# Routed tiles of a mixture of experts: turned by the load's DMA instead of on TensorE

## The chip, the core and the metric

The kernel runs on one core of a Trainium2 chip. A core has TensorE (PE, the 128x128 matrix engine, which writes into PSUM), VectorE (DVE), ScalarE (ACT), GpSimd (POOL) and SyncE (SP, which here only issues transfers), and 16 DMA engines that they share. The engines run side by side and wait for one another through semaphores. The metric is the device time of one execution in microseconds; less is better.

## What is computed

A cross-attention block and then a transformer block with a mixture of experts, for 16 sequences of 128 tokens of width 256 (2,048 tokens). The change touches only the experts that a token is sent to. For each token the four largest of 16 routing weights are taken; each of the token's four experts computes a gated product, and the results are summed by weight:

```python
logits = x2 @ gate_w.T
probs = softmax(logits)
top_w, top_i = top_k(probs, 4); top_w = top_w / sum(top_w)
gu = einsum('th,eih->tei', x2, w1)          # 16 experts, 352 columns: gate | up
act = silu(gu[..., :176]) * gu[..., 176:]
down = einsum('tei,ehi->teh', act, w2)      # back to width 256
routed = einsum('te,teh->th', wfull, down)  # wfull: top_w at top_i, else 0
```

## The kernel before

Every float32 operand is split into a high and a low half of 16 bits, and a product is three products of halves (`three`, lines 666 to 670: high by high, high by low, low by high).

The kernel first does the attention of all sequences, group after group of four. While it does so, POOL scatters the rows of the tokens into a table `xg` in memory, sorted by expert (line 1536): a row holds the token's 256 high halves, its 256 low halves, and for the 16 experts the destination and the weight as 32 words, 1,152 bytes together. A short stage for the shared experts' products follows, and then the stage that the change touches.

That stage takes the sorted rows in 80 slots of 128 rows (tiles), 79 of them in use, each of one expert; two tiles are a pair, and 40 pairs (`PAIRS`) are worked through. For pair u:

- SP loads the pair's tiles from `xg` into one of four buffers `xin` (`load`, line 637; the issue is line 644). It may do so when TensorE has turned the pair four before (`tx_free`) and DVE has written that pair's destinations (`idx`).
- TensorE turns them (`turn_tile`, line 1067): the products need the 256 columns on the partitions, so four 128x128 blocks a tile are transposed into one PSUM bank (line 1076), and DVE copies them to `xt`, of which there are two (`take`, line 2118, the copy is line 2123).
- DVE picks the destination and the weight of the pair's expert out of the 32 words (`select`, lines 2130 and 2135) and later writes them where the scatter and the store read them (`index`, lines 2144 and 2145), when POOL has seen the scatter of the pair four before land (`y_free`).
- TensorE makes gate and up (`gate_up`, line 1086, 12 products a pair through lines 668 to 670).
- ACT takes tanh of the gate (line 1408), DVE multiplies twice (`expert`, lines 2150 and 2152), ACT cuts the product to its high half (line 1414), DVE makes the low half (`lo_tile`, lines 2157 and 2158).
- TensorE turns the product (`turn_m`, line 1107), ACT copies it (line 1420), TensorE makes the down products (`down_tile`, lines 668 to 670, 1119 and 1120), ACT stores them times the weight (line 1428), and POOL scatters the rows to their destinations in `y4` (`send`, line 1594).

Each engine has its own fixed order, written out by hand. TensorE for pair u: gate and up of u, turn of u+2, down of u-2, turn of the product of u-1. ACT: tanh of u, cut of u, copy of u-1, store of u-2. DVE: the two multiplications of u, index of u, copy of u+2 (`take`), selection for u+2, low part of u. After the last pair SP loads `y4` back, and DVE adds the four results of each token and the rest.

Of the kernel before, what the change touches and what calls it, by code (L numbers as in the profile page):

```python
# [9 lines left out]
F32, F16, BF16 = mybir.dt.float32, mybir.dt.float16, mybir.dt.bfloat16  # L10
U32, I32 = mybir.dt.uint32, mybir.dt.int32

P = 128
NB, S, D = 16, 128, 256
KC = D // P
# [7 lines left out]
NE, EI, TOPK = 16, 176, 4  # L23
# [6 lines left out]
GU = 2 * EI  # L30
# [19 lines left out]
PAIRS = NT // 2  # L50
# [5 lines left out]
RW = 2 * D + 4 * NE  # L56
# [8 lines left out]
CH = SHL * NC  # L65
TC = 17
HID = 2048
ATT = HID + 1024
# [61 lines left out]
def build(nc, x, yT, wa, wall, cst, ident, maskb, pad, xg, y4, zb, x1d, x2t, out):  # L130
    assert (WRES - NH * HW) % SMALL == 0 and sum(CUTS) == NH
    with ExitStack() as ctx:
# [5 lines left out]
        def sem(name):  # L138
            if name not in sems:
                sems[name] = ctx.enter_context(nc.semaphore(name))  # L140
            return sems[name]
# [9 lines left out]
        def apart(eng):  # L151


            eng.sem_inc(sem("apart"), 1)
# [36 lines left out]
        idn, tri, ones = (idn2[:, n * P:(n + 1) * P] for n in range(3))  # L191

        def words(a, n):
            return ar[:, a:a + n]

        def halves(a, n):
            return ar[:, a:a + n].bitcast(F16)

        def bank16(b, n=1):
            return ps[:, b:b + n, :].rearrange("p b w -> p (b w)").bitcast(F16)  # L200

        def bank(b, n=1):
            return ps[:, b:b + n, :].rearrange("p b w -> p (b w)")
# [136 lines left out]
        def wcol(w, off, n=P):  # L340
            return w[:, bass.ds(off, n)]
# [20 lines left out]
        nt_i = tab[:, 4 * NT + 3 * NE:4 * NT + 4 * NE].bitcast(I32)  # L362
        grid = words(ATT, NT * NE).rearrange("p (t e) -> p t e", e=NE)
        up16 = words(ATT + NT * NE, NE * NE).rearrange("p (f e) -> p f e", e=NE)
        xin = [halves(ATT + RW * b, RW).rearrange("p (i c) -> p i c", i=2) for b in range(4)]
        xinw = [words(ATT + RW * b, RW).rearrange("p (i c) -> p i c", i=2) for b in range(4)]
        xt = [halves(ATT + 4 * RW + 512 * b, 512).rearrange("p (l k t) -> p l k t", l=2, k=KC) for b in range(2)]
        m_t = [words(ATT + 3328 + 448 * b, 2 * EI).rearrange("p (i n) -> p i n", i=2) for b in range(2)]
        m_p = [words(512 * b, 2 * EI).rearrange("p (i n) -> p i n", i=2) for b in range(2)]
        m_s = [halves(RT + 384 * b, 384).rearrange("p (i n) -> p i n", i=2) for b in range(2)]  # L370
# [3 lines left out]
        selw = [words(ATT + 4224 + 72 * b, 72) for b in range(2)]  # L374
        yb = [(whi, wlo)[m // 4][:, LATE0 + 4096 * (m % 4):LATE0 + 4096 * (m % 4 + 1)].bitcast(F32) for m in range(NB // 2)]
        ob = [words(ATT + 512 * m, 512) for m in range(NB // 2)]
        GUB, TXB, MB, DB = (0, 2), 4, 5, (6, 7)
        gate_ps = [ps[:, GUB[b]:GUB[b] + 2, 0:EI] for b in range(2)]
        up_ps = [ps[:, GUB[b]:GUB[b] + 2, EI:GU] for b in range(2)]

# [65 lines left out]
        def unit_at(slot):  # L446

            return slot - slot // 3 if slot % 3 != 2 and slot < SMALL * 3 // 2 else None
# [24 lines left out]
        def tiles(u):  # L473

            return min(2, LIVE - 2 * u)
# [12 lines left out]
        def _(sp):  # L488
# [82 lines left out]
            for p in range(LAST):  # L571
# [20 lines left out]
                if p >= FIRST:  # L592
                    g, t = divmod(p - FIRST, GB)
                    if t == 2:
                        load_x1(g)
                    for n in range(GB):
                        u = unit_at((p - FIRST) * GB + n)
# [38 lines left out]
            def load(u, v, again=True):  # L636

                if again:
                    sp.wait_ge(sem("tx_free"), u + 1)
                    sp.wait_ge(sem("idx"), u - 3)  # L640
                both = sp.value_load(rowtab[0:1, u:u + 1], min_val=0, max_val=512 * 512 - 1)
                for i, r in enumerate((both & 511, both >> 9)[:tiles(u)]):
                    r = (r * P).with_bounds(min_val=0, max_val=SLOTS - P)
                    sp.dma_start(xinw[v][:, i, :], xg[bass.ds(r, P), :]).then_inc(sem(f"xin{v}"), 16)

            for u in range(PAIRS):
                load(u, u % 4, u >= 4)
# [14 lines left out]
        def _(pe):  # L662
# [3 lines left out]
            def three(o, l_hi, l_lo, r_hi, r_lo, start, stop):  # L666

                mm(o, l_hi, r_hi, start=start, stop=False, skip_group_check=True)  # L668
                mm(o, l_hi, r_lo, start=False, stop=False, skip_group_check=True)  # L669
                return mm(o, l_lo, r_hi, start=False, stop=stop, skip_group_check=True)  # L670
# [389 lines left out]
            s_down(2, 2)  # L1060

            pe.wait_ge(sem("fin"), SHL)
            pe.sem_inc(sem("tx_free"), 4)
            pe.sem_inc(sem("u_ps"), 2)
            pe.sem_inc(sem("d_ps"), 2)

            def turn_tile(u, v, n):

                pe.wait_ge(sem(f"xin{v}"), n)
                pe.wait_ge(sem("tx_bank"), u + 1)  # L1070
                t = bank16(TXB).rearrange("p (l k t) -> p l k t", l=2, k=KC)
                for i in range(tiles(u)):
                    for l in range(2):
                        for k in range(KC):
                            o = (l * KC + k) * P
                            last = nc.tensor.transpose(t[:, l, k, i * P:(i + 1) * P], xin[v][:, i, o:o + P], idn)  # L1076
                last.then_inc(sem("tx_free"), 1)

            word = {}

            def fetch(n):

                if n < NT // 4:
                    word[n] = pe.value_load(exptab[0:1, n:n + 1], min_val=0, max_val=16 ** 4 - 1)

            def gate_up(u, b):

                off = [((word[u // 2] >> 4 * (2 * (u % 2) + i)) & 15) * ES + LATE0 for i in range(2)]
                pe.wait_ge(sem("tx_bank"), u + 2)
                pe.wait_ge(sem("me_v"), u + (CH + 2))  # L1090
                for i in range(tiles(u)):
                    tt = slice(i * P, (i + 1) * P)
                    for k in range(KC):
                        last = three(bank(GUB[b] + i)[:, 0:GU], xt[b][:, 0, k, tt], xt[b][:, 1, k, tt],
                                     wcol(whi, off[i] + k * GU, GU), wcol(wlo, off[i] + k * GU, GU),
                                     k == 0, k == KC - 1)
                last.then_inc(sem("u_ps"), 1)
                return off

            def turn_m(u, b):  # L1100

                pe.wait_ge(sem("me_lo"), u + (CH + 3))
                pe.wait_ge(sem("mT_cut"), u)
                o = bank16(MB)[:, 0:6 * P].rearrange("p (c i t) -> p c i t", c=3, i=2)
                for i in range(tiles(u)):
                    for n in range(3):
                        last = nc.tensor.transpose(o[:, n, i, :], m_s[b][:, i, n * P:(n + 1) * P], idn)  # L1107
                last.then_inc(sem("mt_ps"), 1)
# [14 lines left out]
            pe.wait_ge(sem("stage_cut"), NH + SMALL + 1 + LATE)  # L1123
            pe.wait_ge(sem("table"), 3)
            fetch(0)
            for u in range(2):
                turn_tile(u, u, 32)
            off = {}
            for u in range(PAIRS + 2):
                if u < PAIRS:  # L1130
                    off[u] = gate_up(u, u % 2)
                if u + 2 < PAIRS:
                    turn_tile(u + 2, (u + 2) % 4, 32 * ((u + 2) // 4) + 16 * tiles(u + 2))
                if u % 2:
                    fetch(u // 2 + 1)
                if u >= 2:
                    down_tile(u - 2, u % 2, off[u - 2])
                if 1 <= u <= PAIRS:
                    turn_m(u - 1, (u - 1) % 2)
# [477 lines left out]
        def _(dve):  # L1617
            prime(dve, "dve")
            V = nc.vector
# [491 lines left out]
            s_add(2)  # L2111
            r_z(g)

            dve.sem_inc(sem("tx_bank"), 1)
            dve.sem_inc(sem("me_lo"), 1)
            dve.sem_inc(sem("me_v"), 2)

            def take(u, b):

                dve.wait_ge(sem("tx_free"), u + 5)  # L2120
                dve.wait_ge(sem("u_ps"), u + (CH + 1))
                apart(dve)
                V.tensor_copy(xt[b].rearrange("p l k t -> p (l k t)"), bank16(TXB)).then_inc(sem("tx_bank"), 1)

            def select(u, v, n):

                b = v % 2
                dve.wait_ge(sem(f"xin{v}"), n)
                for i in range(2):
                    last = STT(selw[b][:, 32 * i:32 * i + 32].rearrange("p (w e) -> p w e", w=2),  # L2130
                               cs[:, C_IOTA:C_IOTA + NE].unsqueeze(1).broadcast_to([P, 2, NE]), etab[:, 2 * u + i:2 * u + i + 1],
                               xinw[v][:, i, D:D + 2 * NE].rearrange("p (w e) -> p w e", w=2), ALU.is_equal, ALU.mult)
                last.then_inc(sem("dve_step"), 1)
                dve.wait_ge(sem("dve_step"), 2 * u + (NG * RC + TC + 1))
                V.tensor_reduce(selw[b][:, 64:68], selw[b][:, 0:64].rearrange("p (i e) -> p i e", i=4),
                                AX.X, ALU.add).then_inc(sem("dve_step"), 1)
# [24 lines left out]
            for b in range(2):  # L2161
                V.memset(m_s[b][:, :, EI:2 * P], 0.0)
            for u in range(2):
                take(u, u)
                select(u, u, 32)
            for u in range(PAIRS):
                expert(u, u % 2)
                index(u, u % 4)
                if u + 2 < PAIRS:
                    take(u + 2, u % 2)  # L2170
                    select(u + 2, (u + 2) % 4, 32 * ((u + 2) // 4) + 16 * tiles(u + 2))
                lo_tile(u, u % 2)

# [125 lines left out]
```

## Time and the profile before

| | |
|---|---|
| time before, median of three runs | 987.31 us (984.85 to 988.54) |
| span of the profiled execution | 989.1 us |
| time of the profiled execution outside its span | not given |
| mean granted TensorE clock | 0.910 |
| instructions | 24,025 |
| DMA | 83.81 MB, 85 GB/s on average |

The span is the time from the first to the last instruction. The clock is given as a share of full speed, 2.4 GHz. In the rows of the profile, L1076 is line 1076 of the kernel; PE is a product on TensorE, PEld its load of weights; SPq is SP's queue. `ar`, `ps`, `whi` and `wlo` are the names of buffers: `ar` holds nearly all that is worked on, `ps` is PSUM, `whi` and `wlo` the weights' halves. A bracket such as [0.77 <-ACT ar L1408] says how long the engine stood idle ahead of the instruction and what ended the wait. Matmuls are pipelined, so their lengths overlap; the distance from one start to the next is the rate.

### The profile page before, as it was taken

How to read it: one execution, taken by the hardware profiler on the slowest of the kernel's cores; microseconds unless marked ns; L12 is line 12 of the kernel's file. 1: busy time of each engine (PE TensorE's matmuls, PEld its weight loads, DVE VectorE, ACT ScalarE, POOL GpSimd, SP SyncE). 2: the span in 40 equal slices, each digit the busy share in tenths (PEclk: the TensorE clock that was granted, in tenths of full speed). 3: DMA queues.
4: the chain of work that ended last, by engine and by line, in shares of the span. 5: the costliest groups of instructions: out<-in, count | busy, mean ns of one | idle time of the engine just before them, and what ended most of it. 6: DMA issues, size and time to landing. Idle time of an engine off the chain costs nothing. (4 is left out here: it accounts for less than half of the span.)

```text
span 989.1 us, 24025 instructions
## 1 busy us (share of the span) xinstructions
PE 861.2 (87%) x8118; PEld 611.6 (62%) x8118; DVE 794.5 (80%) x2309; ACT 664.4 (67%) x1611; POOL 516.8 (52%) x607
## 2 busy tenths in 40 slices
PE   3476689999999898999999899998998579999971
PEld 1243346777767676676767677676765357787740
DVE  4688878888888988989998877778867767777738
ACT  3677878888888877788788676666753136666640
POOL 5778883466466463777745264211453715554540
PEclk8555559999999999999999999999999779999986
DMA  5222320101001010122000223114231534444448
GB/s 183 93 77 75 102 104 23 31 19 43 15 25 30 23 52 1 59 87 71 26 15 9 65 91 119 39 34 134 80 103 46 189 108 150 153 155 148 137 161 316
DMA packets 47493, 83.81 MB, mean 85 GB/s; under 512 B 6144, under 2 KB 36224, under 8 KB 47328
## 3 DMA queue, kind: packets, MB, share of 16 engines
q1 hardware_dynamic: 39504, 61.45, 19.7%
q0 software_dynamic: 6864, 19.80, 5.7%
q8 instruction: 69, 1.13, 0.5%
q10 hardware_dynamic: 1008, 1.03, 0.3%
q14 instruction: 48, 0.39, 0.1%
HBM read 52.77 MB, written 31.85 MB: 86 GB/s over the span
## 5 line engine op out<-in xcount | busy, mean ns | idle before, releaser
L668 PE MATMUL ps<-whi,ar 128*128 128x256 f16 (+1 forms) x797 | 225.9, 283 | 19.0 <-DVE ar L1764 9.4
L670 PE MATMUL ps<-whi,ar 128*128 128x256 f16 (+1 forms) x797 | 225.6, 283 | 0.0
L669 PE MATMUL ps<-wlo,ar 128*128 128x256 f16 (+1 forms) x797 | 225.6, 283 | 0.0
L1543 POOL TENSOR_TENSOR ar<-ar,sm 128x512 f32<-128x512 f32 x64 | 69.8, 1090 | 149.2 <-DVE sm L1833 149.1
L668 PE MATMUL ps<-ar 128*128 128x128 f16 (+1 forms) x768 | 117.4, 207 | 13.0 <-issue 5.3
L1458 POOL TENSOR_TENSOR sm<-sm,mhalf 128x1 f32<-128x1 f32 (+2 forms) x72 | 125.4, 1741 | 6.0
L1594 POOL DMA_INDIRECT y<-ar,idx x79 | 76.0, 962 | 88.3 <-ACT ar L1428 74.4
L669 PE MATMUL ps<-ar 128*128 128x128 f16 (+1 forms) x768 | 117.0, 206 | 0.0
L670 PE MATMUL ps<-ar 128*128 128x128 f16 (+1 forms) x768 | 117.0, 206 | 0.0
L668 PE MATMUL ps<-ar,whi 128*128 128x512 f16 x292 | 114.3, 392 | 0.2
L669 PE MATMUL ps<-ar,whi 128*128 128x512 f16 x292 | 114.2, 391 | 0.0
L670 PE MATMUL ps<-ar,wlo 128*128 128x512 f16 x292 | 113.9, 390 | 0.0
L668 PEld LDWEIGHTS ps<-whi,ar 128*128 128x128 f16 x797 | 78.6, 99 | 43.3 <-DVE ar L1764 10.2
L1507 POOL TENSOR_TENSOR ar<-ar 128x512 f16<-128x512 f32 x64 | 78.6, 1230 | 49.9 <-ACT ar L1212 49.8
L1268 ACT ACTIVATE ar<-ps 128x512 f16<-128x512 f32 x128 | 76.8, 601 | 34.7 <-PE ps L670 33.4
L1799 DVE SCALAR_TENSOR_TENSOR ar<-ps,ar 128x512 f16<-128x512 f32 x128 | 86.3, 678 | 15.8 <-ACT ar L1268 14.6
L1292 ACT ACTIVATE ar<-ps,sm 128x128 f32<-128x128 f32 x256 | 90.7, 377 | 0.8
L668 PEld LDWEIGHTS ps<-ar 128*128 128x128 f16 x768 | 72.1, 98 | 28.4 <-issue 19.6
L670 PEld LDWEIGHTS ps<-whi,ar 128*128 128x128 f16 x797 | 78.6, 99 | 15.8
L669 PEld LDWEIGHTS ps<-wlo,ar 128*128 128x128 f16 x797 | 78.5, 99 | 15.5
L1536 POOL DMA_INDIRECT xg<-xrow,rn x64 | 67.7, 1057 | 16.8 <-issue 15.6
L1826 DVE CUSTOM_DVE_ANT_0 ps<-ps,msk 128x128 f32<-128x128 f32 x256 | 66.3, 320 | 12.3 <-PE ps L670 11.2
(234 smaller groups left out, 2308.0 us busy)
## 6 DMA issues: line engine op xcount, KB each, us to landing
ar<-xg SPq DMA_DIRECT2D x79, 144.0 KB
ar<-in_wall SPq DMA_DIRECT2D x16, 512.0 KB, 3.6
stg<-in_wall SPq DMA_DIRECT2D x32, 188.0 KB, 2.5
ar<-in_wall SPq DMA_DIRECT2D x8, 608.0 KB, 4.3
whi<-y SPq DMA_DIRECT2D x4, 1024.0 KB, 8.1
wlo<-y SPq DMA_DIRECT2D x4, 1024.0 KB, 16.0
xg<-in_pad SPq DMA_DIRECT2D x1, 2304.0 KB
xg<-x1d SPq DMA_DIRECT2D x4, 512.0 KB, 4.7
```

Of the source, the lines that this page charges most:

```text
L668: mm(o, l_hi, r_hi, start=start, stop=False, skip_group_check=True)
L669: mm(o, l_hi, r_lo, start=False, stop=False, skip_group_check=True)
L670: return mm(o, l_lo, r_hi, start=False, stop=stop, skip_group_check=True)
L1268: A(qkT[:, w, 0, :], bank(QKV[b]), ACT.Copy, scale=(-QK_SCALE, QK_SCALE)[w]).then_inc(sem(("q_hi", "k_hi")[w]), 1)
L1292: last = A(pr[:, j, :], bank(SB_)[:, j * S:(j + 1) * S], ACT.Exp, bias=nm4[:, j:j + 1], scale=-1.0, accum_out=es4[:, j:j + 1])
L1458: TT(out, tmp, mhalf[:, 0:w], ALU.pow).then_inc(sem(name + "_rs"), 1)
L1507: TT(to[:, 1].rearrange("p h q -> p (h q)"), of, to[:, 0].rearrange("p h q -> p (h q)"), ALU.subtract).then_inc(sem("xa_pl"), 1)
L1536: nc.gpsimd.indirect_dma_start(out=xg, out_offset=bass.IndirectOffsetOnAxis(ap=pos[:, n:n + 1], axis=0), in_=xrow[:, (n // TOPK) * (RW // ...
L1543: TT(pr, pr, er4.unsqueeze(2).broadcast_to([P, GB, S]), ALU.mult).then_inc(sem("p_n"), 1)
L1594: nc.gpsimd.indirect_dma_start(out=y4, out_offset=bass.IndirectOffsetOnAxis(ap=idx[:, 2 * v + i:2 * v + i + 1], axis=0), in_=ybuf[v][:, i, ...
L1799: STT(qkT[:, w, 1, :], bank(QKV[b]), (-QK_SCALE, QK_SCALE)[w], qkT[:, w, 0, :], ALU.mult, ALU.subtract).then_inc(sem(("q_lo", "k_lo")[w]), 1)
L1826: last = V.tensor_tensor_reduce(bank(SB_)[:, c], bank(SB_)[:, c], msk[:, :], 1.0, -MASKED, ALU.add, ALU.min, nm4[:, j:j + 1])
```

## The change

SP's load of a tile becomes two DMAs. The first, a transposing one, reads the 512 halves of each of the tile's 128 rows and writes them with columns on partitions, straight into `xt`, of which there are now four. The second reads the 32 words of destinations and weights of each row into `xmeta`. TensorE's `turn_tile` and DVE's `take` go; `gate_up` waits for the load itself, and a buffer is free for the next load when `gate_up` of the pair four before is done.

```diff
-        xin = [halves(ATT + RW * b, RW)... for b in range(4)]
-        xinw = [words(ATT + RW * b, RW)... for b in range(4)]
-        xt = [halves(ATT + 4 * RW + 512 * b, 512)... for b in range(2)]
+        xmeta = [words(ATT + 4 * NE * b, 4 * NE).rearrange("p (i c) -> p i c", i=2) for b in range(4)]
+        xt = [halves(ATT + 16 * NE + 512 * b, 512).rearrange("p (l k t) -> p l k t", l=2, k=KC) for b in range(4)]
+        xt_c = [halves(ATT + 16 * NE + 512 * b, 512).rearrange("p (c t) -> p c t", c=2 * KC) for b in range(4)]
+        xg16 = xg.bitcast(F16)
...
             def load(u, v, again=True):
                 if again:
-                    sp.wait_ge(sem("tx_free"), u + 1)
+                    sp.wait_ge(sem("u_ps"), u + (CH - 1))
                     sp.wait_ge(sem("idx"), u - 3)
...
-                    sp.dma_start(xinw[v][:, i, :], xg[bass.ds(r, P), :]).then_inc(sem(f"xin{v}"), 16)
+                    sp.dma_start_transpose(xt_c[v][:, :, i * P:(i + 1) * P], xg16[bass.ds(r, P), 0:2 * D]).then_inc(
+                        sem(f"xin{v}"), 16)
+                    sp.dma_start(xmeta[v][:, i, :], xg[bass.ds(r, P), D:D + 2 * NE]).then_inc(sem(f"xin{v}"), 16)
...
-            def turn_tile(u, v, n):
-                pe.wait_ge(sem(f"xin{v}"), n)
-                pe.wait_ge(sem("tx_bank"), u + 1)
-                t = bank16(TXB).rearrange("p (l k t) -> p l k t", l=2, k=KC)
-                for i in range(tiles(u)):
-                    for l in range(2):
-                        for k in range(KC):
-                            o = (l * KC + k) * P
-                            last = nc.tensor.transpose(t[:, l, k, i * P:(i + 1) * P], xin[v][:, i, o:o + P], idn)
-                last.then_inc(sem("tx_free"), 1)
...
-            def gate_up(u, b):
+            def gate_up(u, b, v, n):
-                pe.wait_ge(sem("tx_bank"), u + 2)
+                pe.wait_ge(sem(f"xin{v}"), 2 * n)
                 pe.wait_ge(sem("me_v"), u + (CH + 2))
-                        last = three(bank(GUB[b] + i)[:, 0:GU], xt[b][:, 0, k, tt], xt[b][:, 1, k, tt],
+                        last = three(bank(GUB[b] + i)[:, 0:GU], xt[v][:, 0, k, tt], xt[v][:, 1, k, tt],
...
-                if u + 2 < PAIRS:
-                    turn_tile(u + 2, (u + 2) % 4, 32 * ((u + 2) // 4) + 16 * tiles(u + 2))
...
-            def take(u, b):
-                dve.wait_ge(sem("tx_free"), u + 5)
-                dve.wait_ge(sem("u_ps"), u + (CH + 1))
-                V.tensor_copy(xt[b].rearrange("p l k t -> p (l k t)"), bank16(TXB)).then_inc(sem("tx_bank"), 1)
             def select(u, v, n):
-                dve.wait_ge(sem(f"xin{v}"), n)
+                dve.wait_ge(sem(f"xin{v}"), 2 * n)
...
-                               xinw[v][:, i, D:D + 2 * NE].rearrange("p (w e) -> p w e", w=2), ALU.is_equal, ALU.mult)
+                               xmeta[v][:, i, :].rearrange("p (w e) -> p w e", w=2), ALU.is_equal, ALU.mult)
...
-                    take(u + 2, u % 2)
```

## Rows read from the trace of the kernel before

**Rows 1.** The page's busy times, share of the span and instructions of each engine.
```profile
PE 861.2 (87%) x8118; PEld 611.6 (62%) x8118; DVE 794.5 (80%) x2309; ACT 664.4 (67%) x1611; POOL 516.8 (52%) x607
```
**Rows 2.** Groups by line from 740 us on: busy us, mean ns | idle before.
```profile
L2123 DVE COPY ar<-ps 128x1024 f16<-128x1024 f16 x40 | 27.4, 684 | 5.1 <-PE ps L1076 5.0 <-issue 0.2
L1076 PE MATMUL ps<-idn,ar 128*128 128x128 f16 x316 | 25.0, 224 | 7.2 <-DMA ar<-xg 5.8 <-DVE ar L2123 1.3
```
**Rows 3.** Stretches of the stage: length, busy time by engine, clock, DMA share, GB/s.
```profile
858.43:936.57 78.14, 77.72 (x760) 61.47 (x758) 59.80 (x210) 50.54 (x106) 40.29 (x42) 1.00 0.49 150
936.57:943.43 6.86, 6.20 (x59) 4.74 (x57) 4.79 (x16) 4.58 (x11) 3.84 (x4) 1.00 0.19 68
```
**Rows 4.** Timeline of TensorE in one pair: start, length, what.
```profile
817.78 0.31 PE L670 MATMUL ps<-whi,ar 128*128 x1
817.93 0.61 PE L1076 MATMUL ps<-idn,ar 128*128 128x128 f16 x8
818.38 0.27 PE L668 MATMUL ps<-whi,ar 128*128 x1
...
819.81 0.31 PE L668 MATMUL ps<-whi,ar 128*128 x1
```
**Rows 5.** Timeline of ACT in the same pair.
```profile
814.47 0.46 ACT L1408 ACTIVATE ar<-ps 128x352 f32<-128x352 f32 x1
816.08 0.50 ACT L1414 ACTIVATE ar<-ar 128x352 f16<-128x352 f32 x1 [1.14 <-DVE ar L2152]
...
817.17 0.84 ACT L1428 ACTIVATE ar<-ps,wt 128x256 f32<-128x256 f32 x2
818.13 0.46 ACT L1408 ACTIVATE ar<-ps 128x352 f32<-128x352 f32 x1
```
**Rows 6.** Timeline of DVE in the same pair.
```profile
818.63 0.52 DVE L2150 SCALAR_TENSOR_TENSOR ar<-ar,ps 128x352 f32<-128x352 f32 x1 [0.77 <-ACT ar L1408]
...
819.76 0.68 DVE L2123 COPY ar<-ps 128x1024 f16<-128x1024 f16 x1
...
822.29 0.52 DVE L2150 SCALAR_TENSOR_TENSOR ar<-ar,ps 128x352 f32<-128x352 f32 x1 [0.77 <-ACT ar L1408]
```
**Rows 7.** Timeline of ACT in the last pairs.
```profile
936.57 0.46 ACT L1408 ACTIVATE ar<-ps 128x352 f32<-128x352 f32 x1
...
940.01 0.47 ACT L1408 ACTIVATE ar<-ps 128x352 f32<-128x352 f32 x1
...
942.71 0.83 ACT L1428 ACTIVATE ar<-ps,wt 128x256 f32<-128x256 f32 x2
943.43 0.47 ACT L1408 ACTIVATE ar<-ps 128x352 f32<-128x352 f32 x1
```
**Rows 8.** Timeline of TensorE in the last pairs.
```profile
942.95 0.28 PE L668 MATMUL ps<-whi,ar 128*128 x1 [0.66 <-ACT ar L1420]
```
**Rows 9.** DMA queues, 810 to 930 us: packets, MB, share of 16 engines.
```profile
q1 hardware_dynamic: 9327, 9.56, 27.5%
q0 software_dynamic: 3069, 8.39, 20.6%
```
**Rows 10.** The same around a load of 128 rows of 512 bytes, 109.05 to 109.60 us.
```profile
q1 hardware_dynamic: 144, 0.07, 41.6%
```
**Rows 11.** Line 644's instructions on SP: duration ns, smallest, median, largest.
```profile
L644 SPq DMA_DIRECT2D ar<-xg x79: 332/333/1344, 791.9 to 932.3; - x79
```
**Rows 12.** Timeline of all engines where the stage starts.
```profile
791.90 6.16 SPq L644 DMA_DIRECT2D ar<-xg  x8
...
794.75 1.04 PE L1076 MATMUL ps<-idn,ar 128*128 128x128 f16 x8 [5.83 <-DMA ar<-xg]
...
797.61 0.50 PE L668 MATMUL ps<-whi,ar 128*128 x1
```
**Rows 13.** Waits from 780 to 950 us: us in total, times, longest.
```profile
DVE wt L2144 <- POOLq L1601: 1.9, 4, 1.1
```
**Rows 14.** Timeline of POOL in one pair.
```profile
820.08 0.96 POOL L1594 DMA_INDIRECT y<-ar,idx  x1 [0.30 <-issue]
```

More of the change, by code:

```diff
@@ L364, in build @@
         up16 = words(ATT + NT * NE, NE * NE).rearrange("p (f e) -> p f e", e=NE)
-        xin = [halves(ATT + RW * b, RW).rearrange("p (i c) -> p i c", i=2) for b in range(4)]
-        xinw = [words(ATT + RW * b, RW).rearrange("p (i c) -> p i c", i=2) for b in range(4)]
-        xt = [halves(ATT + 4 * RW + 512 * b, 512).rearrange("p (l k t) -> p l k t", l=2, k=KC) for b in range(2)]
+        xmeta = [words(ATT + 4 * NE * b, 4 * NE).rearrange("p (i c) -> p i c", i=2) for b in range(4)]
+        xt = [halves(ATT + 16 * NE + 512 * b, 512).rearrange("p (l k t) -> p l k t", l=2, k=KC) for b in range(4)]
+        xt_c = [halves(ATT + 16 * NE + 512 * b, 512).rearrange("p (c t) -> p c t", c=2 * KC) for b in range(4)]
+        xg16 = xg.bitcast(F16)
         m_t = [words(ATT + 3328 + 448 * b, 2 * EI).rearrange("p (i n) -> p i n", i=2) for b in range(2)]
@@ L376, in build @@
         ob = [words(ATT + 512 * m, 512) for m in range(NB // 2)]
-        GUB, TXB, MB, DB = (0, 2), 4, 5, (6, 7)
+        GUB, MB, DB = (0, 2), 5, (6, 7)
         gate_ps = [ps[:, GUB[b]:GUB[b] + 2, 0:EI] for b in range(2)]
@@ L1062, in _ @@
             pe.wait_ge(sem("fin"), SHL)
-            pe.sem_inc(sem("tx_free"), 4)
             pe.sem_inc(sem("u_ps"), 2)
             pe.sem_inc(sem("d_ps"), 2)
-            def turn_tile(u, v, n):
-                pe.wait_ge(sem(f"xin{v}"), n)
-                pe.wait_ge(sem("tx_bank"), u + 1)
-                t = bank16(TXB).rearrange("p (l k t) -> p l k t", l=2, k=KC)
-                for i in range(tiles(u)):
-                    for l in range(2):
-                        for k in range(KC):
-                            o = (l * KC + k) * P
-                            last = nc.tensor.transpose(t[:, l, k, i * P:(i + 1) * P], xin[v][:, i, o:o + P], idn)
-                last.then_inc(sem("tx_free"), 1)
             word = {}
@@ L1125, in _ @@
             fetch(0)
-            for u in range(2):
-                turn_tile(u, u, 32)
             off = {}
@@ L1130, in _ @@
                 if u < PAIRS:
-                    off[u] = gate_up(u, u % 2)
-                if u + 2 < PAIRS:
-                    turn_tile(u + 2, (u + 2) % 4, 32 * ((u + 2) // 4) + 16 * tiles(u + 2))
+                    off[u] = gate_up(u, u % 2, u % 4, 32 * (u // 4) + 16 * tiles(u))
                 if u % 2:
@@ L2112, in _ @@
             r_z(g)
-            dve.sem_inc(sem("tx_bank"), 1)
             dve.sem_inc(sem("me_lo"), 1)
             dve.sem_inc(sem("me_v"), 2)
-            def take(u, b):
-                dve.wait_ge(sem("tx_free"), u + 5)
-                dve.wait_ge(sem("u_ps"), u + (CH + 1))
-                apart(dve)
-                V.tensor_copy(xt[b].rearrange("p l k t -> p (l k t)"), bank16(TXB)).then_inc(sem("tx_bank"), 1)
             def select(u, v, n):
                 b = v % 2
-                dve.wait_ge(sem(f"xin{v}"), n)
+                dve.wait_ge(sem(f"xin{v}"), 2 * n)
                 for i in range(2):
@@ L2163, in _ @@
             for u in range(2):
-                take(u, u)
                 select(u, u, 32)
```

## The prediction

> **What bounds the kernel now.** I read the page first. TensorE is busy in 87% of the span, far above the other engines [rows 1], but that is an average over stages. The change touches only the stage of the routed tiles, 40 pairs from about 791 to 949 us, so I took the table of stretches next. In its middle TensorE is busy for 77.72 of 78.14 us, at full clock (1.00, the 2.4 GHz level), while DVE has 59.80 and ACT 50.54 [rows 3]. TensorE has no idle time there, so taking work from it should help. How much depends on who is next.
>
> For that I read the timeline of one pair, engine by engine. TensorE: the last product of gate and up starts at 817.78, the eight turns of the pair after next at 817.93, the down products at 818.38, the next gate and up at 819.81 [rows 4]. The turns take 818.38 - 817.93 = 0.45 us. ACT: tanh of one pair starts at 814.47, of the next at 818.13; the period is 3.66 us [rows 5]. In between it does the cut, the copy of the turned products and the store, and before the cut it stands 1.14 us waiting for DVE's two multiplications, every time. The store ends at 817.17 + 0.84 = 818.01, the next tanh starts at 818.13, and the last gate product that it needs ends at 817.78 + 0.31 = 818.09. So ACT, at 60% busy, waits for TensorE by only about 0.1 us. The reader should see this: ACT does its four steps strictly in order, with DVE's 1.14 us inside, and this loop is nearly as long as TensorE's.
>
> How long it is without TensorE the trace shows itself. The last pairs have nothing left to turn. There tanh starts at 936.57, 940.01 and 943.43 [rows 7], 3.44 and 3.42 us apart, and now TensorE waits for ACT, 0.66 us before a down product [rows 8]. The last of them starts 0.11 us before the store's end (942.71 + 0.83 = 943.54): ACT is full. So the pace without turns is 3.43 us: TensorE alone would allow 3.66 - 0.45 = 3.21.
>
> **The change part by part.**
>
> *Turns removed.* 316 transposes [rows 2], 0.45 us a pair of TensorE's time. Worth on the path: 3.66 - 3.43 = 0.23 us a pair, because ACT's loop ends later than TensorE's shortened one. The first two pairs and the last two differ, so I count 35 periods: 35 x 0.23 = 8.0 us. From 814.47 to 936.57 there are 33 periods in 122.10 us, 3.70 on average [rows 5, 7]; the 0.04 above 3.66 comes from a few disturbed pairs, and I leave it in place. Bounds: 0 (ACT doesn't give more) to 35 x 0.45 = 15.8 (ACT follows TensorE fully), and the two measured intervals of 3.43 lie between. TensorE will then idle some 0.2 us a pair; in the stretch of those last pairs it is busy for 6.20 of 6.86 us and the clock is 1.00 [rows 3], so I price the clock at nothing.
>
> *DVE's copy removed.* 40 copies of 0.68 us [rows 2]. DVE isn't on the path: it stands 0.77 us in each pair waiting for tanh [rows 6]. Price nothing; but the cover for anything late on DVE grows from 0.77 to 1.45 us.
>
> *Loads become transposing DMAs.* The trace has none, so this is the unknown. What a plain load costs: in 810 to 930 us the SP queue took 27.5% of the 16 engines' 120 us for 9,327 packets [rows 9]; at 144 packets a load (128 rows and 16 that end it, as in [rows 10]) these are 64.8 loads, 0.51 us of all engines each, 57 ns a packet of 1,152 bytes. The scatter of the results takes 20.6%, two for each pair: 0.206 x 120 / 32 = 0.77 us a pair. Now each of a row's four pieces of 128 halves goes to 128 partitions, so I reckon with pieces of 256 bytes: 512 a tile, 32 for each engine. Below: as dear by the byte as the plain load, 128/144 x 0.51 = 0.45 us a tile. Above: each piece as dear as one packet of 1,152 bytes, 32 x 57 ns = 1.82 us. Nearest row: packets of 512 bytes, 0.55 us x 41.6% over 9 packets for each engine = 25.4 ns [rows 10], so 32 x 25.4 = 0.81 us. I take that, because small packets are the likeness that counts.
>
> The plain row, 0.51 us a load, speaks for cheap tiles [rows 9]; it says nothing of crossing partitions. One rule of the Trainium skill speaks against the change: "VectorE: DVE Perf Modes", section The three transpose paths, gives 1,309 ns for one 128x128 block of 2-byte elements by DMA. An estimate from that page: eight blocks a pair, one behind another, would take 10.5 us, and the sum would end some 260 us above today's time. No trace here shows it; the same mechanism, priced from rows, stands among the rivals.
>
> *The small DMAs.* Two more for each pair, 128 pieces of 128 bytes: below, by the byte, next to nothing; at 25.4 ns a packet 9 x 25.4 = 0.23 us each; above, at 57 ns, 0.51.
>
> *All four on the DMA engines.* 2 x (0.81 + 0.23) + 0.77 = 2.85 us a pair, under 3.43; now it is 2 x 0.51 + 0.77 = 1.79. Lowest 2 x 0.45 + 0.77 = 1.67, highest 2 x (1.82 + 0.51) + 0.77 = 5.43.
>
> *SP's issue.* It issues in order, 0.333 us a DMA [rows 11], some 0.45 with the register work. Four instead of two: 1.8 us a pair, beside 3.43; were each transposing issue as long as the longest plain one (1.344), 3.6, about today's period. SP's wait for the index of the pair four before stands as it was, and its other wait is for gate and up in place of the turns. Nothing else is queued behind these on SP until the stage ends.
>
> *When it is needed.* A load goes out when the index of the fourth pair before is done, and DVE's selection for it comes two periods later, 6.9 us. Two plain tiles landed 794.75 - 791.90 = 2.85 us after the first issue [rows 12]; with two more issues and 2 x 0.3 us more on the engines it is about 4.4. So 2.5 us are in hand, and DVE's 1.45 us behind them: selection stands ahead of the low parts on DVE, and TensorE's turning of the products waits for these.
>
> *The start.* The first gate product started at 797.61, 5.71 us after the first issue [rows 12], behind two turns of about 1 us and two copies. With four issues and a landing it may start 4.4 us after; if the tiles cost their upper bound, about 6.5. I take -0.5, with ends of -1.5 and +1.
>
> **Sum.** -8.0 - 0.5 = -8.5 us. The profiled execution's span is 989.1 us, 1.8 above the median of the runs, 987.31; no other time of that execution is given. I put the difference on the median: 987.3 - 8.5 = 979 us, 0.9% faster.
>
> **Rivals.**
>
> *The DMAs can't keep the pace (slower).* The place is SP's queue: gate and up waits for the tile, all else behind it. It decides where a pair's transfers pass today's 3.66 us: (3.66 - 0.77)/2 - 0.23 = 1.2 us a tile, 2.4 times the plain load. For it: 512 pieces instead of 128, crossing partitions, and a queue in which each small DMA stands behind a tile. Against it: the engines are idle half the time now (0.49) [rows 3], and the 512-byte packets were cheap. At 4.9 us a pair (1.82 a tile) it is 38 x 1.24 = 47 us more, 1,034; at the upper bound 5.43, 38 x 1.77 = 67, 1,054. A form of it: a tile's four blocks pass one behind another, each as dear as a whole plain load, 4 x 0.51 = 2.04 a tile, 2 x (2.04 + 0.23) + 0.77 = 5.31 a pair and 1,050. I give that form 0.10 of this rival's 0.30. It is the one that the page named above would bear out, with a far higher price.
>
> *The scatters land later and take the gain.* DVE's index waits until the scatter of the fourth pair before has landed; already it waited in four pairs, 1.9 us in total [rows 13]. The scatter's second issue ends at 820.08 + 0.96 = 821.04 [rows 14], and the landing comes just in time. Tiles of many small pieces on the same 16 engines could delay it. DVE's 1.45 us hide that much; a landing 1.7 us later costs 0.25 a pair and leaves 987, and 2.5 later gives 1.05 a pair against 3.43: 4.48, or 987 + 38 x 0.82 = 1,018. Against it: a scatter is few and large packets, 0.39 us of engine time each.
>
> *ACT's loop gives nothing.* Then TensorE's 0.45 us turn into waits for ACT and the time is 987. The two intervals of 3.43 speak against it, but they are only two.
>
> **How the numbers follow.** About 0.5% (5 us) is what a measurement of this kernel can tell from no change. Forecast: 0.60, of which 0.50 is faster by over 0.5% and 0.10 is a gain that stays under it. DMAs too slow: 0.30, of which 0.28 slower and 0.02 just hidden. Scatters late or ACT's loop holding: 0.10, of which 0.06 same and 0.04 slower. So faster 0.50, same 0.18, slower 0.32. The forecast's own range is 975 to 984 (start and pace at their ends). The whole range must reach into the slow case: 975 to 1,045 leaves out 0.03 below and about 0.12 above.
>
> **What would show it.** Right: no turns on TensorE in the stage, tanh 3.4 us apart, ACT without a gap between store and tanh, TensorE idle some 0.2 us a pair and waiting for ACT's copy, the stage about 8 us shorter, and everything after it unchanged. Wrong: gate and up waiting for a DMA in every pair, tanh at even distances over 3.66 us, SP's queue full. If instead DVE's index waits for POOL's queue in each pair, the second rival holds; if tanh stays 3.66 us apart with ACT full, the third.

## The result and the profile after

The change makes the kernel slower: 1,034.95 us, median of four runs (1,032.12 to 1,041.13), against 986.08 us (984.52 to 988.54) for the kernel before on the same chip. The ratio is 1.0489, 95% interval 1.0455 to 1.0523. I had forecast 979 us, faster; the time lies in the range of 975 to 1,045, where the first rival put it, though not for that rival's reason.

The profiled execution, the slowest of the four (1,041.13 us), spans 1,039.3 us. Busy times on its page, to be held against [rows 1]:

```profile
span 1039.3 us, 23429 instructions
PE 867.8 (84%) x7802; PEld 596.4 (57%) x7802; DVE 773.8 (74%) x2269; ACT 661.6 (64%) x1611; POOL 513.9 (49%) x607
```

TensorE has 316 instructions fewer, which are the turns, and DVE 40 fewer, the copies. TensorE's busy time still rose by 6.6 us, and the last section comes back to that.

**Where the time went.** tanh (L1394 now) starts 40 times, first at 799.34 and last at 993.60 us, (993.60 - 799.34) / 39 = 4.981 us apart on average. Before it was 801.36 to 943.43, or 3.643. So 39 x 1.338 = 52.2 us were lost in the pairs' pace, 2.0 us won at the start, and 50.2 us is the whole difference of the spans, 1,039.3 - 989.1. Behind the last tanh both traces have the same 45.7 us.

The stretch in the middle of the stage (length, busy time of PE, PEld, DVE, ACT, POOL, clock, DMA share, GB/s), to be held against the first row of [rows 3], and a second, short one inside it:

```profile
830.00:950.00 120.00, 93.68 (x689) 62.68 (x687) 56.13 (x220) 56.34 (x123) 46.28 (x48) 0.93 0.50 113
855.00:862.00 7.00, 5.06 (x31) 3.46 (x32) 3.98 (x16) 2.39 (x5) 2.82 (x4) 0.76 0.41 99
```

No engine is full any more: TensorE 78%, DVE 47%, ACT 47%. Nor are the DMA engines, at 0.50, about the share they had before (0.49). When nothing that computes or moves is full, the next thing to look at is who waits for whom. The waits from 780 to 1,000 us (total, times, longest):

```profile
DVE ar L2108 <- DMA ar<-xg: 103.4, 40, 4.0
ACT ar L1400 <- DVE ar L2130: 94.4, 38, 4.0
...
PE ps L1097 <- DVE ar L2136: 43.6, 26, 3.2
...
PE ps L671 <- DMA ar<-xg: 7.0, 2, 5.9
```

The DMA is waited for in every pair, and by DVE's selection (L2108), not by gate and up (L671, only twice). One such wait on DVE, TensorE and ACT:

```profile
865.54 0.41 DVE L2108 SCALAR_TENSOR_TENSOR ar<-cs,tab,ar 128x32 f32<-128x32 f32 x2 [3.06 <-DMA ar<-xg]
...
866.13 0.42 DVE L2135 TENSOR_TENSOR ar<-ar 128x256 f16<-128x256 f32 x1
866.46 0.25 DVE L2136 TENSOR_TENSOR ar<-ar 128x96 f16<-128x96 f32 x1
866.63 0.52 DVE L2128 SCALAR_TENSOR_TENSOR ar<-ar,ps 128x352 f32<-128x352 f32 x1
```

```profile
866.77 0.51 PE L1097 MATMUL ps<-idn,ar 128*128 128x128 f16 x6 [1.55 <-DVE ar L2136]
```

```profile
867.74 0.50 ACT L1400 ACTIVATE ar<-ar 128x352 f16<-128x352 f32 x1 [3.08 <-DVE ar L2130]
```

DVE stands 3.06 us at the selection for a pair that nobody computes on yet. Behind it in DVE's order are the low part of the current pair (L2135, L2136), for which TensorE's turn of the product waits, and the two multiplications of the next (L2128, L2130), for which ACT's cut waits. One late tile stops three engines.

Why is it late? SP's timeline over one pair, its lines over the stage (smallest, median, longest ns), and what SP itself waited for from 795 to 930 us:

```profile
839.55 1.21 SPq L645 DMA_TRANSPOSE ar<-xg  x1
840.96 0.42 SPq L647 DMA_DIRECT2D ar<-xg  x1
841.56 1.20 SPq L645 DMA_TRANSPOSE ar<-xg  x1
842.95 0.43 SPq L647 DMA_DIRECT2D ar<-xg  x1
844.27 1.21 SPq L645 DMA_TRANSPOSE ar<-xg  x1
```

```profile
L645 SPq DMA_TRANSPOSE ar<-xg x79: 1188/1211/2421, 790.1 to 984.6; - x79
...
L647 SPq DMA_DIRECT2D ar<-xg x79: 389/427/1824, 791.6 to 986.0; - x79
...
L642 SPq TENSOR_LOAD <-tab x40: 268/276/528, 789.3 to 983.8; - x40
```

```profile
SPq L642 <- PE ps L673: 0.8, 2, 0.5
```

SP waits for 0.8 us in these 135 and is never done. Issuing one transposing DMA occupies it for 1.21 us, against 0.333 for the plain load of before [rows 11]. A pair takes 844.27 - 839.55 = 4.72 us on SP alone: 2 x 1.21 + 2 x 0.43 = 3.28 in the four issues and 1.44 in the steps between them (the pair's word, L642, and the addresses). Pairs in which an issue or a word load is stretched bring the average to 4.98. The chain that ended last says the same, by line:

```profile
SPq L645 9%; SPq L647 4%; SPq L642 2%; POOL xg L1522 2%; DMA ar<-xg 1%; PE ps L671 1%; PE ps L672 1%; PE ps L673 1%; DVE ar L2156 1%; DVE ar L2163 1%; DVE whi L2154 0%; DVE wlo L2154 0%; PE ps L1097 0%; DMA xg<-xrow,rn 0%; DVE ar L2108 0%
```

Could the 1.21 us be SP held up by full DMA engines? The queues from 830 to 950 us, to be held against [rows 9], and the first issues of the stage:

```profile
q1 hardware_dynamic: 33066, 7.09, 31.3%
q0 software_dynamic: 2304, 6.29, 17.9%
```

```profile
790.07 1.32 SPq L645 DMA_TRANSPOSE ar<-xg  x1
...
791.59 0.41 SPq L647 DMA_DIRECT2D ar<-xg  x1
792.20 1.20 SPq L645 DMA_TRANSPOSE ar<-xg  x1
```

The first issue of the stage, with no tile in flight ahead of it, is no shorter than the others (1.32).

### The profile page after: what moved, and what is told of

It is laid out like the page before. It is cut to its first block and busy times, and to the rows that moved or that the text cites. A ratio compares the mean times of both kernels' runs of the same rounds, so it can differ in the third digit from the quotient of the medians.

```text
span 1039.3 us, 23429 instructions
## 1 busy us (share of the span) xinstructions
PE 867.8 (84%) x7802; PEld 596.4 (57%) x7802; DVE 773.8 (74%) x2269; ACT 661.6 (64%) x1611; POOL 513.9 (49%) x607
## 5 line engine op out<-in xcount | busy, mean ns | idle before, releaser
L671 PE MATMUL ps<-whi,ar 128*128 128x256 f16 (+1 forms) x797 | 232.7, 292 | 25.9 <-DVE ar L1750 9.6
L672 PE MATMUL ps<-wlo,ar 128*128 128x256 f16 (+1 forms) x797 | 232.1, 291 | 0.0
L673 PE MATMUL ps<-whi,ar 128*128 128x256 f16 (+1 forms) x797 | 231.7, 291 | 0.0
L671 PE MATMUL ps<-ar 128*128 128x128 f16 (+1 forms) x768 | 117.3, 207 | 13.6 <-issue 5.3
L671 PEld LDWEIGHTS ps<-whi,ar 128*128 128x128 f16 x797 | 80.3, 101 | 63.6 <-issue 22.4
L671 PE MATMUL ps<-ar,whi 128*128 128x512 f16 x292 | 114.5, 392 | 0.2
L2108 DVE SCALAR_TENSOR_TENSOR ar<-cs,tab,ar 128x32 f32<-128x32 f32 x80 | 16.7, 250 | 103.4 <-DMA ar<-xg 103.4
L673 PEld LDWEIGHTS ps<-whi,ar 128*128 128x128 f16 x797 | 80.6, 101 | 17.3
L671 PEld LDWEIGHTS ps<-ar 128*128 128x128 f16 x768 | 72.1, 98 | 28.8 <-issue 20.0
L1400 ACT ACTIVATE ar<-ar 128x352 f16<-128x352 f32 x40 | 19.9, 497 | 97.3 <-DVE ar L2130 94.4
```

## The experiments

Two theories. A: SP's queue is full, because the issue of a transposing DMA holds it for 1.2 us. B: the transfer itself is slow, small pieces that cross partitions on the DMA engines, as my first rival had it. All kernels start from the changed one. Times are medians, ratios are to the kernel before on the same chip.

**Same pieces, plain DMA.**

```diff
-                    sp.dma_start_transpose(xt_c[v][:, :, i * P:(i + 1) * P], xg16[bass.ds(r, P), 0:2 * D]).then_inc(
+                    sp.dma_start(xt_c[v][:, :, i * P:(i + 1) * P],
+                                 xg16[bass.ds(r, P), 0:2 * D].rearrange("p (c t) -> p c t", t=P)).then_inc(
```

> The transposing DMA is replaced by a plain one of the same rows in the same pieces (256 bytes on both sides), so the tile arrives unturned and the products are made from the wrong layout: only the time is read. Theory A (SP's queue is full, because the issue of one transposing DMA holds SP for 1.2 us): four plain issues of 0.43 us, some 0.2 around each and 0.5 for the table word make about 3.0 us a pair on SP, under ACT's loop of 3.43, so the time is what the prediction said for the removed turns alone, 979 us (975 to 984), with tanh 3.43 us apart. Theory B (the 512 pieces a tile on the 16 DMA engines set the pace, and SP's records are long because the engines push back): the pieces are the same, so at least 1,020 us.

Measured: 975.59 us (973.06 to 976.61), ratio 0.9861 (0.9833 to 0.9889). tanh from 797.21 to 932.10 us, 3.459 apart on average, median 3.42. The issues, and the middle of the stage:

```profile
L645 SPq DMA_DIRECT2D ar<-xg x79: 383/383/1437, 789.5 to 921.4; - x79
```

```profile
800.00:930.00 130.00, 126.75 (x1045) 90.36 (x1046) 86.76 (x340) 83.92 (x184) 67.53 (x71) 1.00 0.61 155
```

The kernel leaves the turning out, so only its time is read. The same number of DMAs, bytes and 256-byte pieces, with another issue: the loss is gone. What is left is the pace that I had forecast, 3.42 for 3.43, with TensorE at full clock. It leaves room for crossing partitions as the price, since these pieces don't cross; the next two kernels settle that.

**Small DMAs issued by ACT.** SP keeps the transposing DMAs and nothing else; ACT issues the small ones behind tanh, three pairs ahead, on semaphores of their own.

```diff
-                    sp.dma_start(xmeta[v][:, i, :], xg[bass.ds(r, P), D:D + 2 * NE]).then_inc(sem(f"xin{v}"), 16)
...
+            def meta(u, v):
+                if u >= 4:
+                    act.wait_ge(sem("idx"), u - 3)
+                both = act.value_load(rowtab[0:1, u:u + 1], min_val=0, max_val=512 * 512 - 1)
+                for i, r in enumerate((both & 511, both >> 9)[:tiles(u)]):
+                    r = (r * P).with_bounds(min_val=0, max_val=SLOTS - P)
+                    act.dma_start(xmeta[v][:, i, :], xg[bass.ds(r, P), D:D + 2 * NE]).then_inc(sem(XM[v]), 16)
```

> The small DMAs are issued from ACT, three pairs ahead, in the 1.1 us that ACT waits for DVE in each pair; the transposing ones stay on SP. Theory A: SP has two issues of 1.2 us, 0.2 around each and about 0.85 for word, waits and registers, 3.65 us a pair instead of 4.7 to 4.9, so 990 to 998 us. Theory B: the same transfers cross the same engines, so it stays near 1,035 (over 1,025). If ACT's queue can't hide the issues, its loop grows to about 4.3 us, 1,010 to 1,020, with ACT and not SP without a gap.

Measured: 983.23 us (981.76 to 985.01), ratio 0.9951 (0.9929 to 0.9972). tanh 3.637 apart on average, median 3.42, from 795.12 to 936.98. The issues, and the queues from 810 to 930 us (q10 is ACT's):

```profile
L646 SPq DMA_TRANSPOSE ar<-xg x79: 1188/1191/2607, 786.7 to 929.1; - x79
```

```profile
q1 hardware_dynamic: 35362, 8.53, 40.8%
q0 software_dynamic: 3105, 8.52, 24.1%
q10 hardware_dynamic: 9310, 1.06, 12.1%
```

The transfers are those of the changed kernel; only the engine that issues the small ones is another, and with it their queue. 51.7 us came back, and the ratio fell from 1.0489 to 0.9951. The 79 issues, 786.7 to 929.1 us, are 142.4 / 78 = 1.83 us apart, 3.65 a pair, which is what theory A gave for SP, and tanh keeps that average. The engines were busier than in the changed kernel, 0.77 (the sum of the three rows) against 0.50, at a much better pace: they had not been the limit. The time itself is a miss: it lies under A's 990 to 998 us, although A's pace held. The range did not follow from that pace, since 39 x (4.98 - 3.65) = 51.9 us off 1,034.95 is 983. The stage also began earlier here (first issue at 786.7, not 790.1), for a reason that I don't know.

**Each transposing DMA cut in two**, of 64 rows each.

```diff
-                    sp.dma_start_transpose(xt_c[v][:, :, i * P:(i + 1) * P], xg16[bass.ds(r, P), 0:2 * D]).then_inc(
-                        sem(f"xin{v}"), 16)
+                    for h in range(2):
+                        sp.dma_start_transpose(xt_c[v][:, :, i * P + HALF * h:i * P + HALF * h + HALF],
+                                               xg16[bass.ds(r + HALF * h, HALF), 0:2 * D]).then_inc(sem(f"xin{v}"), 16)
```

> Each transposing DMA is split into two of 64 rows; pieces and bytes stay the same. Theory A: the issue on SP decides. If its 1.2 us is a fixed price, four of them with 0.2 each, two small ones and the word make 7.7 us a pair, about 1,145 us; if it goes by the blocks moved, 0.6 each, about 5.2 us a pair and 1,050 to 1,060; so in either case slower than the change, by how much tells the fixed part. Theory B: the same pieces, the same time, 1,035 (1,028 to 1,042).

Measured: 1,139.78 us (1,138.48 to 1,141.40), ratio 1.1528 (1.1496 to 1.1560), tanh 7.505 apart on average. The issues, and the queues from 830 to 1,070 us:

```profile
L646 SPq DMA_TRANSPOSE ar<-xg x158: 1169/1176/2292, 791.7 to 1088.6; - x158
```

```profile
q1 hardware_dynamic: 45648, 9.38, 20.0%
q0 software_dynamic: 3001, 8.17, 10.1%
```

Half the rows cost SP 1.18 us instead of 1.21: the price goes by the DMA, not by its bytes. It decides between the theories, for the bytes are unchanged, the engines are no busier, and the time is 105 us longer.

**One tile of each pair turned by DMA, the other on TensorE.** Tile 0 keeps the transposing and the small DMA, tile 1 comes by the plain load of before, with four turns and half a copy, so that SP has one dear issue a pair. All three DMAs of a pair count on one semaphore.

```diff
+                if tiles(u) == 2:
+                    sp.dma_start(xinw[v], xg[bass.ds(rows[1], P), :]).then_inc(sem(f"xin{v}"), 16)
+                for i, r in enumerate(rows[:1]):
...
+                for l in range(2):
+                    for k in range(KC):
+                        o = (l * KC + k) * P
+                        last = nc.tensor.transpose(t[:, l, k, :], xin[v][:, o:o + P], idn)
```

> Of each pair one tile comes by the transposing DMA with its small DMA, the other by the plain load of before and four turns on TensorE with half the copy on DVE. Theory A: SP needs 0.43 + 1.4 + 0.6 + 0.85 = 3.3 us a pair, TensorE 3.66 - 0.22 = 3.44, ACT 3.43, so about 981 us (977 to 988), faster than both kernels. Theory B: transport of 0.5 + 2.4 us or so a pair would also fit in 3.44, so it says the same here; a time over 1,000 would speak against A.

Measured: 997.65 us (993.77 to 1,003.78), ratio 1.0097 (1.0066 to 1.0129), a miss. About half of the pairs go at 3.44 (the median is 3.53), but the average is 3.964: some take 4.3 to 7.55. The waits of the turn from 795 us on, and one of them on TensorE with ACT's copy behind it:

```profile
PEld ps L1082 <- DMA ar<-xg: 15.6, 17, 2.1
...
PE ps L1082 <- DMA ar<-xg: 9.6, 12, 1.7
```

```profile
846.19 0.40 PE L1082 MATMUL ps<-idn,ar 128*128 128x128 f16 x4 [1.41 <-DMA ar<-xg]
```

```profile
849.91 0.81 ACT L1433 ACTIVATE ar<-ps 128x768 f16<-128x768 f16 x1 [3.00 <-PE ps L1115]
```

The turn of the plain tile stood in front of the down products and waited for all three landings, the transposing one too, which it doesn't need. The next kernel tests that reading.

**The plain tile on a semaphore of its own.**

```diff
-                pe.wait_ge(sem(f"xin{v}"), n)
+                pe.wait_ge(sem(XP[v]), XP0[v] + 16 * (u // 4 + 1))
```

The turn also moves behind the down products on TensorE.

> As the version with one transposed tile a pair, but the plain tile counts on a semaphore of its own, so TensorE's turn and DVE's copy no longer wait for the transposing and the small DMA of the same pair, and the turn stands behind the down products. Theory A (that version kept ACT's pace of 3.44 in most pairs and lost its 0.5 us a pair to the turn waiting for three landings): the waits of the turn for a DMA (25 us there) go, and with SP at 3.3 us a pair the time is 978 to 985 us. Theory B (two kinds of transfers disturb each other on the DMA engines): the pace stays irregular, 3.9 us on average, and the time near 997.

Measured: 983.89 us (981.49 to 986.57), ratio 0.9961 (0.9948 to 0.9974). Average 3.664, median 3.44.

```profile
PEld ps L1084 <- DMA ar<-xg: 7.8, 10, 1.4
...
DVE ar L2152 <- DMA ar<-xg: 6.6, 11, 0.9
PE ps L1084 <- DMA ar<-xg: 5.2, 6, 1.1
```

The wait for the landing is about halved and 14 us came back; own semaphore and later place were changed together, so their shares are not told apart. SP still has no slack: it waited for DVE's destinations by 0.9 us in the whole stretch of 795 to 945 us.

**The same, with the small DMA issued by ACT**, one a pair, as in the second kernel.

> The same with the small DMA issued from ACT three pairs ahead, one a pair. Theory A: SP then needs only 0.34 + 0.2 + 1.2 + 0.2 + 0.85 = 2.8 us a pair, 0.6 below ACT's loop, so late issues are caught up: 974 to 981 us, the fastest of the correct ones. If SP at 3.3 us was enough already, the same as the run before it within 3 us.

Measured: 981.15 us (972.90 to 982.66), ratio 0.9920 (0.9890 to 0.9949). Average 3.555, median 3.44. SP's own waits, then those for the landing, 795 to 930 us:

```profile
SPq L646 <- DVE idx L2182: 22.8, 26, 1.8
```

```profile
DVE wt L2181 <- POOLq L1631: 12.3, 13, 2.8
...
PEld ps L1084 <- DMA ar<-xg: 1.0, 1, 1.0
```

Now SP waits for DVE, 22.8 us, as an issuing queue should: it has slack. Waits for a landing are nearly gone. This version computes all that the kernel computes and beats the kernel before by 0.8% and the changed one by about 5%; its median lies just past the upper end of what I expected (981). The second kernel, whole and with the small DMAs on ACT too, gained 0.5%; the intervals of the two overlap (0.9929 to 0.9972 and 0.9890 to 0.9949), so which is better isn't shown.

## Why the prediction was wrong

- **The step that failed is "SP's issue"**: "1.8 us a pair, beside 3.43", and at worst 3.6. It measured 4.72. Two sizes were off. The transposing issue, which no row of before shows, was bounded by the longest plain one (1.344); it is 1.21 in the median, so that bound was good, but I took the plain median. And "0.45 with the register work" left 0.12 us beside each issue, a size for which I gave no row, where 1.44 / 4 = 0.36 is needed. In the kernel with plain pieces four cheap issues already take 841.30 - 838.27 = 3.03 us of SP a pair, as the lines under this list show. With 0.36 in place of 0.12 the worst case would have been 2 x 1.344 + 2 x 0.333 + 1.44 = 4.8 us, past 3.66, and a case to be priced. A row of before spoke of it, and I read it for another purpose: SP's first eight plain issues take 6.16 us [rows 12], or (6.16 - 0.33) / 7 = 0.83 apiece at the start of the stage, not 0.45.
- **The first rival had the place right and the price from the wrong resource.** It put the loss in SP's queue but reckoned the DMA engines' time; its 1,034 us at 4.9 us a pair is near the measured 4.98 only by chance. Of its marks SP's full queue was seen, but not gate and up waiting in every pair nor tanh at even distances (they are 3.42 to 7.49 us). DVE's selection waits instead; its semaphore counts all four DMAs, so that it waits for the small one, issued last, is likely but not shown.
- **The DMA engines' sum held.** 2.85 us a pair were reckoned; measured are 0.50 x 4.98 = 2.5 in the changed kernel and 0.77 x 3.64 = 2.8 with the small DMAs on ACT's queue. There a transposed tile takes 0.408 x 120 / 65 = 0.75 us of all engines (0.81 reckoned) and a small DMA 0.121 x 120 / 63 = 0.23 (0.23). The page "VectorE: DVE Perf Modes" of the Trainium skill, section The three transpose paths, has 1,309 ns for one block by DMA. An estimate from that page is 10.5 us a pair for eight in a row; with the small DMAs on ACT eight pass in 3.65, so at that price they don't go one behind another. The page "Advanced Engine Details and Errata" of the Trainium skill, section X-Bar Transpose (TRN2), calls transposing DMAs as fast as regular ones; these runs don't agree, neither on the engines (0.75 us a tile against 0.51 for the plain load, which has more bytes) nor on the issue (1.21 against 0.333).
- **The turns were worth what was forecast.** Without them and with a queue that keeps up, tanh comes 3.42 us apart, ACT's loop sets it, and TensorE at 126.75 of 130 us keeps full clock, as I priced it, though it idles less than I reckoned (3.25 of 130 us, about 0.09 a pair and not 0.2). In the plain kernel the pace gives (3.643 - 3.459) x 39 = 7.2 us, where 8.0 were forecast. It gains 4.2 us more by an earlier first tanh and 3.0 us behind the last (974.8 - 932.10 = 42.7, not 45.7). I can't assign the first. The second goes with TensorE's granted clock and not with the turns: in the first 20 us behind the last tanh the clock is 1.00 in the plain kernel, but 0.78 for 8 us and 0.86 for 12 both before and in the changed kernel, and the slow version with 64 rows a DMA has 1.00 and 42.7 us there too.
- **The start.** The first gate product comes 795.60 - 790.07 = 5.53 us after the first issue, where I had 4.4 and before it was 5.71; the stage's own beginning moved by 1.8.
- **The second rival exists, small here, and is what is left at the end.** Where the median is 3.42 to 3.44, DVE waits for the scatter's landing 12 to 15 us in 12 to 19 pairs (12.3 in 13 in the last version), against 1.9 in 4 [rows 13]. In the plain kernel it is 13.8 us in 16 pairs, and the pace is 3.459 all the same, so most of it is covered. In the last version it isn't: two pairs take 5.26 and 5.87 us, with waits of 2.59 and 2.82 us for a landing, and these two make 4.25 of the 4.5 us by which its 39 periods exceed 3.44.

SP in the kernel with plain pieces, the first issue of one pair and of the next:

```profile
838.27 0.38 SPq L645 DMA_DIRECT2D ar<-xg  x1
...
841.30 0.38 SPq L645 DMA_DIRECT2D ar<-xg  x1
```

## What to carry to other kernels

Reckon an issuing queue like an engine: sum all its steps for one period, the register work and the word loads too, take them from a stretch in which the queue runs freely, and give a kind of DMA that the trace lacks a price of its own for the issue, apart from its price on the DMA engines. When a trace shows no engine full and the DMA engines half idle, look at the queue that issues. Work that is off the critical path can be swapped against a wait on it: here 0.23 us a pair were to be won, and SP's 4.72 us a pair were the price. Once the issues fitted, the swap paid a little: 0.5% for both tiles with the small DMAs on another queue, 0.4% for one tile of each pair, 0.8% for both measures together.

## What the runs showed of the hardware

- The issue of a transposing DMA costs SP 1.18 us for 64 rows and 1.21 for 128 rows of 1,024 bytes, a plain one of the same shape and pieces 0.38, one of 128 bytes a row 0.43 (0.36 in the kernel with plain pieces).
- Single issues stretch: up to 2.42 us in the changed kernel, 2.61 with the small DMAs on ACT and 2.98 in the last version. They come together with transfers of 16 KB on the queue that the profile calls q8 instruction, one for about every three pairs: of the issues on SP that are over 0.3 us longer than the median of their line, 66 of 67 in the eight traces of this case overlap such a transfer, and of the 961 others 57 do. Whether it causes the stretch no run tested. A full queue doesn't make such issues up: with the small DMAs on ACT the median is 3.42 and the average 3.637. Slack on SP doesn't remove them either. In the last version one issue (its length, then the queues during it, 859.36 to 862.25 us) is followed by a late landing of a scatter; q1's packets take 97.0% of the engines' time there, against 36.9% in 810 to 930 us:

```profile
859.36 2.89 SPq L652 DMA_TRANSPOSE ar<-xg  x1
```

```profile
q1 hardware_dynamic: 578, 0.26, 97.0%
...
q8 instruction: 1, 0.02, 4.2%
```

```profile
863.63 0.17 DVE L2181 COPY wt<-ar 128x2 f32<-128x2 f32 x1 [2.59 <-POOLq L1631]
```

- Behind a long wait TensorE's clock fell. In 855 to 862 us, with a wait of 1.99 us that ended at 856.94, the granted clock is 0.76; it is 0.50 in 859 to 861, where products start 0.29 to 0.30 us apart (half speed, 1.2 GHz), and 1.00 again from 862, where it is 0.15 (2.4 GHz). TensorE's busy time rose by 6.6 us although it does less, and all of it lies between the first issue and the last tanh (152.52 us against 145.95). I put it down to the clock, 0.93 against 1.00 in the middle of the stage; no run tested it apart:

```profile
856.94 0.51 PE L1097 MATMUL ps<-idn,ar 128*128 128x128 f16 x6 [1.99 <-DVE ar L2136]
...
859.05 0.50 PE L671 MATMUL ps<-whi,ar 128*128 x1
859.35 0.50 PE L672 MATMUL ps<-wlo,ar 128*128 x1
...
862.17 0.31 PE L671 MATMUL ps<-whi,ar 128*128 x1
862.32 0.31 PE L672 MATMUL ps<-wlo,ar 128*128 x1
```
